# A four-layer graph network: the work between its edge loops as one stage by groups of three bins

## The reference

```python
h = maximum(_layernorm(x), 0);  x = x + _L0_gnn_ref(h, ...)   # edge network, sum over dst
h = maximum(_layernorm(x), 0);  x = x + _L1_gnn_ref(h, ...)   # attention, 4 heads, ELU scores, segment softmax
h = maximum(_layernorm(x), 0);  x = x + _L2_gnn_ref(h, ...)   # attention, 8 heads, leaky ReLU scores, + bias
h = maximum(_layernorm(x), 0);  x = x + _L3_gnn_ref(h, ...)   # 16 relations: h @ w_self.T + sum of h[dst] @ weights[type]
# L1:  xp = h @ W;  s_src = sum_f xp * a_src;  s_tgt = sum_f xp * a_tgt   (per head)
#      e = elu(s_src[src] + s_tgt[tgt]);  out = segment_sum(softmax(e) * xp[src])
```

## Time and profile before

| | us |
|---|---|
| runs shown, median (lowest, highest) | 4807.97 (4806.36, 4817.33) |
| profiled execution, its own time | 4812.4 |
| its span, first to last instruction | 4810.7 |
| mean granted TensorE clock, share of full | 0.642 |
| busy in the span: TensorE matmul | 3498.6 (73%) |
| VectorE | 2713.0 (56%) |
| ScalarE | 1320.5 (27%) |
| GpSimd | 3322.3 (69%) |

### The profile page before, as it was taken

One profiled execution on the slowest core, in us unless ns is written; L12 is line 12 of the kernel. 1 busy time (PEld: TensorE's weight loads), 2 busy tenths in 40 slices (PEclk: granted clock), 3 DMA queues, 4 the chain that ended last, 5 costly groups with the idle time before them and its releaser, 6 DMA issues. The chain is left out here.

```text
span 4810.7 us, 82491 instructions
## 1 busy us (share of the span) xinstructions
PE 3498.6 (73%) x18822; PEld 2823.9 (59%) x18822; DVE 2713.0 (56%) x8356; ACT 1320.5 (27%) x4613; POOL 3322.3 (69%) x3348
## 2 busy tenths in 40 slices
PE   4999999998488888787738988888968333443433
PEld 2555555554377777777727878888864333333333
DVE  6677777666356556666675666666564433333332
ACT  4444444443244444444422222222212000000000
POOL 4777777775577777777507777777750777777776
PEclk8999999999555555555555555555559555555555
DMA  4555444450344343333312223332215222222222
GB/s 93 111 106 97 90 88 88 89 90 16 102 99 101 98 101 97 98 97 96 66 28 56 77 72 76 81 85 60 56 40 219 53 52 51 52 53 51 52 52 57
DMA packets 489853, 378.45 MB, mean 79 GB/s; under 512 B 307089, under 2 KB 442043, under 8 KB 486316
## 3 DMA queue, kind: packets, MB, share of 16 engines
q0 software_dynamic: 106496, 184.24, 17.1%
q1 hardware_dynamic: 383144, 192.14, 16.7%
HBM read 327.50 MB, written 33.83 MB: 75 GB/s over the span
## 5 line engine op out<-in xcount | busy, mean ns | idle before, releaser
L1054 POOL DMA_INDIRECT mlp_row<-tab,mlp_index x832 | 840.5, 1010 | 308.0 <-issue 243.0
L1054 POOL DMA_INDIRECT gat_row<-tab,gat_index x832 | 847.8, 1019 | 293.4 <-issue 224.9
L1054 POOL DMA_INDIRECT rel_row<-tab,rel_index x832 | 808.4, 972 | 255.2 <-issue 231.7
L1054 POOL DMA_INDIRECT att_row<-tab,att_index x832 | 803.6, 966 | 253.4 <-issue 249.1
L1446 PE MATMUL rel_ps_sum<-rel_row,rel_hot 128*128 128x128 f32 x1664 | 426.2, 438 | 649.3 <-DMA rel_row<-tab,rel_index 649.3
L1446 PEld LDWEIGHTS rel_ps_sum<-rel_row,rel_hot 128*128 128x128 f32 x1664 | 370.7, 328 | 705.4 <-DVE rel_hot L1471 414.1
L1676 PE MATMUL gat_ps_sum<-gat_row,gat_hot 128*128 128x136 f32 x1664 | 443.1, 448 | 179.0 <-ACT gat_sums L1625 128.5
L1872 PE MATMUL att_ps_sum<-att_row,att_hot 128*128 128x136 f32 x1664 | 446.1, 448 | 116.1 <-DVE acc L1357 112.3
L1676 PEld LDWEIGHTS gat_ps_sum<-gat_row,gat_hot 128*128 128x128 f32 x1664 | 389.1, 331 | 193.4 <-ACT gat_hot L1619 122.5
L1357 DVE TENSOR_TENSOR acc<-acc,rel_ps_sum 128x128 f32 x416 | 119.5, 287 | 666.8 <-PE rel_ps_sum L1446 637.0
L1872 PEld LDWEIGHTS att_ps_sum<-att_row,att_hot 128*128 128x128 f32 x1664 | 381.7, 326 | 191.8 <-DVE acc L1357 187.7
(11 more groups left out here) (276 smaller groups left out, 6087.0 us busy)
## 6 DMA issues: line engine op xcount, KB each, us to landing
mlp_aim<-in_dst SPq DMA_DIRECT2D x416, 128.0 KB
gat_aim<-in_dst SPq DMA_DIRECT2D x416, 128.0 KB
mlp_row<-in_edge_attr SPq DMA_DIRECT2D x416, 64.0 KB
tab<-n_stage SPq DMA_DIRECT2D x25, 1024.0 KB
mlp_row<-tab,mlp_index POOLq DMA_INDIRECT x832
gat_row<-tab,gat_index POOLq DMA_INDIRECT x832
att_row<-tab,att_index POOLq DMA_INDIRECT x832
rel_row<-tab,rel_index POOLq DMA_INDIRECT x832
```

What stands on the lines that cost most here:

```text
L1054: gp.indirect_dma_start(rows[n][b][:, t, :], None, tables[n], bass.IndirectOffsetOnAxis(index[b][:, n, t:t + 1], axis=0)).then_inc(s_g[b], 16)
```

## The change

`finish` and `node_phase` of one boundary become one stage, with one barrier fewer. All work goes by `THREE`, nine groups of three bins (the last has one). A class `Norm` holds residual, statistics (VectorE `bn_stats` and `bn_aggr` in place of sums, differences and squares), root and normed row (ScalarE, one instruction a bin: Relu(x * scale + bias)), and a clear of `g.acc` by GpSimd behind the residual of each group; the loops' own memsets and waits for them are gone.

In layers 1 and 2 the weights get 2 x 4 or 2 x 8 columns more, made once at the start from weights and score vectors, so that one product of 136 or 144 columns gives row and both scores. ScalarE copies them out in three pieces a group. The table is sent in three parts. In layer 3 the five products of a bin go through four banks and the transposes have one bank; residual, scales, scan and the transposes of later groups stand between the bins. The final addition goes by five chunks of five bins, each with its own DMA.

```diff
+THREE = [range(a, min(a + 3, N_BINS)) for a in range(0, N_BINS, 3)]
+class Norm:
+    def begin(self, v):                       # layers 2, 3: denominators, one pass
+        self.ch.do(v.scalar_tensor_tensor(self.den, total, 0.0, total, ALU.is_equal, ALU.add))
+        self.ch.do(v.reciprocal(self.den, self.den))
+    def residual(self, v, n):
+        if self.layer == 1:
+            for a in THREE[n]:
+                ins = v.scalar_tensor_tensor(g.X[:, a, :], g.bn2[:], g.acc[:, a, D:D + 1], g.X[:, a, :],
+                                             ALU.mult, ALU.add)
+            ch.do(ins)
+            ch.do(v.tensor_tensor(g.X[:, here, :], g.X[:, here, :], g.acc[:, here, 0:D], ALU.add))
+        else:
+            if self.layer == 3:
+                v.tensor_tensor(g.X[:, here, :], g.X[:, here, :], bias2 ..., ALU.add)
+            for a in THREE[n]:
+                ins = v.tensor_tensor(g.TMP[:, a, :] ..., self.sums[:, a, :, 0:self.f], self.den[:, a, :] ..., ALU.mult)
+            ch.do(ins)
+            ch.do(v.tensor_tensor(g.X[:, here, :], g.X[:, here, :], g.TMP[:, here, :], ALU.add))
+        v.sem_inc(self.s_fin, 1)
+    def scan(self, v, n):
+        for a in THREE[n]:
+            ins = v.bn_stats(self.stats[:, a, :], self.g.X[:, a, :])
+        self.ch.do(ins)
+        for a in THREE[n]:
+            ins = v.bn_aggr(self.mv[:, a, :], self.stats[:, a, :])
+        ins.then_inc(self.s_var, 1)
+    def deviation(self, act, n):
+        act.wait_ge(self.s_var, n + 1)
+        act.activation(self.g.std[:, here], self.mv[:, here, 1], ACT.Sqrt, bias=self.eps[:]).then_inc(self.s_std, 1)
+    def scales(self, v, n):
+        v.wait_ge(self.s_std, n + 1)
+        self.ch.do(v.reciprocal(self.g.var[:, here], self.g.std[:, here]))
+        v.scalar_tensor_tensor(self.g.mu[:, here], self.mv[:, here, 0], -1.0, self.g.var[:, here],
+                               ALU.mult, ALU.mult).then_inc(self.s_rstd, 1)
+    def apply(self, act, n):
+        act.wait_ge(self.s_rstd, n + 1)
+        for a in THREE[n]:
+            ins = act.activation(g.H[:, a, :], g.X[:, a, :], ACT.Relu, bias=g.mu[:, a:a + 1], scale=g.var[:, a:a + 1])
+        ins.then_inc(self.s_h, 1)
+    def clear(self, gp):
+        for n, bins in enumerate(THREE):
+            gp.wait_ge(self.s_fin, n + 1)
+            gp.memset(self.g.acc[:, span(bins), :], 0.0)
+def attention_nodes(nc, g, layer, tables):
+        def _(v):        # VectorE
+            v.tensor_copy(w[:, 0:D], g.w1[:] if layer == 1 else p_w[:, 0:D]) ...
+            for side in range(2):
+                ins = v.tensor_tensor(prod[:, side], by_head, rows[:].rearrange(order, h=heads)[:, side], ALU.mult)
+            v.tensor_reduce(w[:, D:wide].rearrange("p (s h) -> p s h", s=2), prod[:], AX.X, ALU.add).then_inc(s_wc, 1)
+            norm.begin(v)
+            for n in range(len(THREE)):
+                norm.residual(v, n)
+                if n:
+                    norm.scales(v, n - 1)
+                norm.scan(v, n)
+            norm.scales(v, len(THREE) - 1)
+        def _(act):      # ScalarE
+            for n in range(len(THREE) + 3):
+                apply(n - 1); deviation(n); keep_three(n - 2)
+                if 0 <= n - 3:
+                    act.wait_ge(s_m, m + 1)
+                    act.copy(stage[:, here, :, 0:f], made[:, :, 0:D] ...)
+                    act.copy(source scores ...); act.copy(g.tgt[:, here, 0:heads], made[:, :, D + heads:wide]).then_inc(s_mc, 1)
+        def _(pe):       # TensorE
+            for n in range(len(THREE)):
+                turn_three(pe, g, norm, p_t, n, s_tc, s_t)
+                if n:
+                    send(n - 1)          # three products of `wide` columns, banks m0 and m1 in turn
+            send(len(THREE) - 1)
+        def _(sp):       # SP
+            for n in range(2, len(THREE), 3):
+                sp.wait_ge(s_mc, n + 1)
+                sp.dma_start(rows[:, here, :], whole[:, here, :]).then_inc(s_row, 16)
+def relation_nodes(nc, g, tables):
+        ring, banks = 3, 4
+        def _(v):        # VectorE
+            norm.begin(v); residual(0); scan(0); residual(1); scales(0); scan(1)
+            for a in range(N_BINS):
+                next(tables_s, None)     # from a = 1
+                for part in (0, 2, 4): ...    # X += bank, two copies, as before
+                m = a // 3
+                if a % 3 == 0 and m + 1 < len(THREE):
+                    norm.scales(v, m + 1)
+                if a % 3 == 0 and m + 2 < len(THREE):
+                    norm.residual(v, m + 2)
+                if a % 3 == 1 and m + 2 < len(THREE):
+                    norm.scan(v, m + 2)
+        def _(act):      # ScalarE: copies of parts 1 and 3, then
+                if a % 3 == 0: norm.apply(act, m + 1)
+                if a % 3 == 1: keep_three(act, ht, p_t, m + 1, s_t, s_tc)
+                if a % 3 == 2: norm.deviation(act, m + 2)
+        def _(pe):       # TensorE: out() of part n waits for the copy of part n - 4
+                if a % 3 == 1: turn_three(pe, g, norm, p_t, a // 3 + 1, s_tc, s_t)
-def finish(nc, g, layer, out=None):
+def finish(nc, g, out):
+            for bins in chunks:
+                v.tensor_tensor(g.X[:, here, :], g.X[:, here, :], g.acc[:, here, 0:D], ALU.add).then_inc(s_sum, 1)
...
-            gp.memset(g.acc[:, :, 0:D], 0.0).then_inc(s_init, 1)
-            v.wait_ge(s_init, 1)
```

More of the change, by code:

```diff
@@ new lines, in _ @@
+            send(len(THREE) - 1)
+        @block.gpsimd
+        def _(gp):
+            if layer == 1:
+                gp.memset(stage[:, :, :, f], 1.0).then_inc(s_one, 1)
+            norm.clear(gp)
+        @block.sync
+        def _(sp):
+            if layer == 1:
+                sp.wait_ge(s_one, 1)
+            rows = tables.rearrange("(a n) f -> n a f", a=N_BINS)
+            for n in range(2, len(THREE), 3):
+                here = slice(THREE[n - 2][0], THREE[n][-1] + 1)
+                sp.wait_ge(s_mc, n + 1)
+                sp.dma_start(rows[:, here, :], whole[:, here, :]).then_inc(s_row, 16)
+            sp.wait_ge(s_row, 48)
@@ new lines, in _ @@
+            for _ in tables_s:
+                pass
+        @block.scalar
+        def _(act):
+            norm.deviation(act, 0)
+            norm.apply(act, 0)
+            keep_three(act, ht, p_t, 0, s_t, s_tc)
+            norm.deviation(act, 1)
+            for a in range(N_BINS):
+                for part in (1, 3):
+                    n = 5 * a + part
+                    act.wait_ge(s_m, n + 1)
+                    if part == 1 and a >= ring:
+                        act.wait_ge(s_out[a % ring], 16 * (a // ring))
+                    act.copy(stage[:, a % ring, (part - 1) * 512:part * 512], p_m[n % banks][:]).then_inc(s_ma, 1)
+                m = a // 3
+                if a % 3 == 0 and m + 1 < len(THREE):
+                    norm.apply(act, m + 1)
+                if a % 3 == 1 and m + 1 < len(THREE):
+                    keep_three(act, ht, p_t, m + 1, s_t, s_tc)
+                if a % 3 == 2 and m + 2 < len(THREE):
+                    norm.deviation(act, m + 2)
@@ L986, in _ @@
+        @block.gpsimd
+        def _(gp):
+            norm.clear(gp)
         @block.sync
         def _(sp):
[L988 to L999 removed]
+            rows = tables.rearrange("(a n r) f -> a n (r f)", a=N_BINS, n=P)
+            for a in range(N_BINS):
+                sp.wait_ge(s_mc, 3 * a + 3)
+                sp.wait_ge(s_ma, 2 * a + 2)
+                sp.dma_start(rows[a], stage[:, a % ring, :]).then_inc(s_out[a % ring], 16)
+            for n in range(ring):
+                sp.wait_ge(s_out[n], 16 * len(range(n, N_BINS, ring)))
@@ new lines, in _ @@
+            for bins in chunks:
+                here = span(bins)
+                v.tensor_tensor(g.X[:, here, :], g.X[:, here, :], g.acc[:, here, 0:D], ALU.add).then_inc(s_sum, 1)
+        @block.sync
+        def _(sp):
+            for n, bins in enumerate(chunks):
+                last = min(bins[-1] + 1, FULL)
+                sp.wait_ge(s_sum, n + 1)
+                sp.dma_start(out[bins[0] * P:last * P, :].rearrange("(a b) f -> b a f", b=P),
+                             g.X[:, bins[0]:last, :]).then_inc(s_o, 16)
+            sp.dma_start(out[FULL * P:N_NODES, :], g.X[0:LAST, FULL, :]).then_inc(s_o, 16)
+            sp.wait_ge(s_o, 16 * (len(chunks) + 1))
@@ L1537, in _ @@
         def _(gp):
-            gp.memset(g.acc[:], 0.0).then_inc(s_init, 1)
             pipeline(gp, [(0, gather_stages(None, gp, *io, WIDE)[1])], WIDE)
@@ L1821, in _ @@
         def _(gp):
-            gp.memset(g.acc[:, :, 0:W], 0.0).then_inc(s_init, 1)
             pipeline(gp, [(0, gather_stages(None, gp, *io)[1])])
```

360 lines of the change are left out of this document (152 added, 208 removed).

## The result

Four executions of the changed kernel took 4733.02 to 4749.68 us, median 4738.26; four of the kernel before took 4806.36 to 4817.33, median 4809.41. The ratio is 0.985, 95% interval 0.983 to 0.9875: faster by 1.5%, 71 us by the medians. Forecast were 4740 and a range of 4725 to 4766.

The account below looks back on a forecast made before the run. Between loops one VectorE queue was taken as the bound, in boundary 3's products TensorE. Terms -22.6 - 25.3 - 17.9 - 2.7 = -68.5 us took the profiled 4812.4 to 4743.9, about 4740 by the median; range 4725 to 4766.

Parts of the forecast that it names:

- Boundaries 1 and 2: Attention stages after loops 1 and 2: VectorE's queue at 2.93 us a group; first gathers 22.6 and 25.3 us earlier.
- price of the scan: Attention stages: three bn_stats and three bn_aggr a group cost VectorE 1.25 us, bounds 0.4 to 2.2.
- tail of 4.2: Boundaries 1 and 2, last copy to next stage: uncovered transfer of the table's last seven bins, 4.2 us (3.0 to 4.84).
- The rule against small tiles: Skill's advice for tiles of 512 or more: 128-wide instructions would cost 6 us over both attention stages; forecast set it aside.
- Boundary 3: Relation stage after loop 3: first product 29.2 us earlier, less what the products then cost more, net -17.9 us.
- the stalls: Relation stage: TensorE waits 0.95 us for a bank in seven groups, +6.7 us (0 to 14).
- the walk of the banks: Relation stage: VectorE frees product 0's bank at 3.7 us, TensorE gets there at 2.8, so it stalls 0.95.
- Rival (c): Relation stage: stalls cost TensorE its full clock, +91 us at 1.2 GHz, so 4831, slower than before; chance 0.04.
- (a): Attention stages slower than 2.93 a group, by dear bn_stats or bn_aggr or ScalarE as bound: 4753 us; chance 0.17.
- (b): Relation stage loses more, 2.4 us a group, VectorE late in the second bin too: 4751 us; chance 0.13.
- (d): Gain mostly given back in loops that end no earlier, leaving the time within 0.3%; chance 0.03.
- (e): Better than forecast, with cheap bn_stats and no stall: -12 us, so 4728; chance 0.05.

Follow-up runs that it names:

- e3: Changed kernel with the attention scores made by VectorE from the table's rows again, not copied from the product; ratio 0.998 to the kernel before.
- e7: Changed kernel with three more bn_stats a group in the two attention stages, into an unread buffer; 5855 us, kernel before 5910.
- e8: Changed kernel with one more ScalarE copy of 384 elements out of PSUM a group in the attention stages; 4751 us, kernel before 4818.
- e11: e9 with the attention stages' addition into X on GpSimd and VectorE's scan put ahead of the scales; 5842.0 us, ratio 0.989 to the kernel before.
- e9: Changed kernel with the edits of e5 and e4, and the attention tables sent in four pieces, the last of one bin; 5830.3 us, kernel before 5909.1.
- e2: Changed kernel with acc cleared by one memset at each loop's start again, not by groups; ratio 0.9945 to the kernel before.
- e5: Changed kernel with VectorE's work in the relation stage spread between the bins in small pieces; ratio 0.990 to the kernel before.
- e4: Changed kernel with the two sums of the source table asked of TensorE after bin 12, not bin 10; 5848 us, kernel before 5910.
- e6: Changed kernel with two more 384-wide VectorE copies behind each residual of the relation stage; 5838 us, kernel before 5910.
- e0: The changed kernel run again without an edit; 5925.7 us, kernel before 5977.8, ratio 0.991.
- e10: Changed kernel with the attention addition into X on GpSimd and, after bin 12, three pairs of source-table sums; 4743.6 us, ratio 0.985 to the kernel before.
- e1: Changed kernel with the old relation stage, the sum ahead of it and the last loop's memset put back; ratio 0.994 to the kernel before.

## Why the prediction was right

The median came out within 2 us of the forecast. The mechanism held, but so close an agreement is in part luck: terms err in both directions, the boundaries and the end give -67.6 for -68.5, and by the two profiles, loops included, the kernel gained 62.8.

- **Boundaries 1 and 2** (forecast -22.6, -25.3; measured -24.2, -26.8). The mechanism held: VectorE's queue sets the period (e3, e7), ScalarE lies just below (e8). The price of the scan was too high: bn_stats takes 0.28 alone and 0.19 behind others, bn_aggr 0.18 and 0.07, three of each 0.93 in VectorE's queue, not 1.25. The residual of the first stage was too low, 1.58 and not 1.38: a scalar_tensor_tensor takes 0.35 and 0.25, more than the products it was priced by. So a group took 2.81 and 2.63 for 2.93. ScalarE was priced at 2.8 at full length and 2.5 overlapped, and needs 2.2 (e11). The tail of 4.2 was right in size (4.1; 4.1 to 5.1 in the second boundary) but not in kind: it was taken as part of a transfer's time, and with a last piece of a seventh of the size it stayed (e9, e11).
- **The rule against small tiles** was rightly put aside: the three 128-wide products of the second stage take 0.69, as the earlier trace rows say, and the period leaves no room for more.
- **First gather 2.6 and 2.7 earlier** for the memsets: e2 gives 3.1 and 2.5.
- **Boundary 3** (-17.9; -13.9). First product -29.4 for -29.2; from the last table transfer on -0.3. The products' stretch grew by 15.9 where 11.3 was forecast. The transposes took 2.2 for 2.6, by e11, which has neither stall nor fall; the low clock at the start 2.8 for 2.0; the stalls 4.8 for 6.7, six of 0.37 to 1.03 rather than seven of 0.95. Not in the sum were 0.9 more wait at the sums (1.11, where it was 0.22 before) and 3.4 for the fall, half of 6.8. Another 1.8 are left. In e5, without stalls, the same terms add up to the measured 101.2, so what is left hangs on the stalls, some 0.3 for each beyond its own length; why stays open. The step that failed is the order of the source table's items: they come one a bin on VectorE, and the walk of the banks was made for the products and not for the two sums, which ask for these items after bin 10. Asked for after bin 12, they are there, and the wait and the fall are gone (e4).
- **Rival (c)** was written as a clock lost to stalls. It came in small, one fall of 6.8 us and not the whole stage. Single stalls of up to 2.2 leave the grant at 1.00 (e6), so the premise that any gap in the row of products costs the clock was wrong. With two sums a fall came only where the wait of 1.1 stood before them, mostly close behind a stall, and in e0, e2 and e6 before the first sum had begun. Six sums brought one without a wait (e10). The forecast had no term for any of this.
- **The end**: -2.7, as forecast.
- **Rivals (a), (b), (d), (e)**: (a) is refuted by e7 and e8, (b) by the stalls' own sizes, (d) by loops 2 and 3, which are no longer than before on the first kind of chip (e1). Of (e), bn_stats were cheap indeed, at half the gain priced there; the stalls came.

What stays open: loop 4 took 1066.2 us before and 1075.5, 1075.6 and 1072.2 in three profiles of the new kernels on chips of that kind; the mean of its gathers on GpSimd is 983, 983 and 979 ns against 972, while loop 2's is 1019 to 1022 in all four. On the other kind of chip the loop behind the old relation stage (e1) took 1252 and behind the new ones 1240 to 1262, the gathers 965 to 970 in all. One profile of before isn't enough to call it an effect; if it is one, it takes back 6 to 9 of the 71 us.

## What to carry to other kernels

Between two stages that can't overlap, price the queue of the busiest engine instruction by instruction, and look for work that another engine does for nothing: here 8 or 16 more columns of a product that TensorE makes anyway were worth 41 of the 51 us of the two attention boundaries, the memsets some 5.6, and all the rest of the change some 4. Where several engines hand buffers round, spread what one of them does between its copies in pieces shorter than the slack of a bank, and walk every waiting item past the new order, the small ones too. Before work is moved from VectorE to GpSimd, look at what will stand beside it: next to instructions with one input it was free, next to one with two it cost what it saved.

## What the runs showed of the hardware

- GpSimd's addition of 384 elements with both inputs in SBUF takes 0.99; a VectorE scalar_tensor_tensor beside it waits until it ends (0.80 for 0.16), bn_stats, bn_aggr, reciprocal don't.
- TensorE's grant stayed at 1.00 behind single stalls of up to 2.2 us between products (e6). It fell to 0.50 for 6.8 us in a wait of 1.1 that stood close behind a stall of 0.9 to 2.05, before the next matmul had begun (e0_again, e2, e6), and after 3.4 us of gapless matmuls with 25 rows (e10).
- In the first boundary the time from the last copy to the next stage was 3.9 and 4.2 us with a last transfer of 68 KB (e9, e11) and 4.1 with one of 476 KB.
- In boundary 1 the grant swung between 0.50 and 1.00 and moved the period not at all, but in e0_again, e1, e2 and e9 a low stretch fell on the last products, and the last copy came 0.8 to 1.0 later than in the changed kernel.
